# Second attention of a four-layer model: attention outputs and their sums leave PSUM by ACT, are inverted once per sequence on DVE and multiplied on POOL

## The reference, cut to what matters

```python
qkv = x @ w_attn
q = qkv[..., :D].reshape(Bv, Tv, H, HEAD_D).transpose(0, 2, 1, 3)
k = qkv[..., D:D + HEAD_D]
v = qkv[..., D + HEAD_D:]
att = jnp.einsum('bhqd,bkd->bhqk', q, k) * scale
att = jnp.where(causal[None, None, :, :], att, -jnp.inf)
att = jax.nn.softmax(att, axis=-1)
y = jnp.einsum('bhqk,bkd->bhqd', att, v)
y = y.transpose(0, 2, 1, 3).reshape(Bv, Tv, D)
return y @ w_proj
```

## Time and profile before

| | |
|---|---|
| median of 3 runs | 796.57 us (796.4 to 796.59) |
| span of the profiled execution, first to last instruction | 801.9 us; no other time of that execution is listed |
| PE busy / DVE busy | 644.6 us (80%) / 548.5 us (68%) |
| ACT busy / POOL busy | 353.9 us (44%) / 361.2 us (45%) |
| attention turns 1 to 6, from one query product to the next | 37.5 to 37.9 us each |

### The profile page before, as it was taken

How to read it: one execution, slowest core, us unless ns; L and a number is a source line. 1 busy time by engine, 2 the same in 40 slices (tenths; PEclk the granted TensorE clock), 3 DMA queues, 4 the chain that set the end, 5 groups by cost and what they waited for, 6 DMA issues and landing times.

```text
span 801.9 us, 14622 instructions
## 1 busy us (share of the span) xinstructions
PE 644.6 (80%) x4312; PEld 398.9 (50%) x4345; DVE 548.5 (68%) x1808; ACT 353.9 (44%) x764; POOL 361.2 (45%) x513
## 2 busy tenths in 40 slices
PE   1489898997206699999795569899999999999795
PEld 1246666664103478877584223454545454544453
DVE  8378888888691133243336797889898989898454
ACT  0323232320711222233231205776777777767883
POOL 0176555552007587788862102434434344333342
PEclk9999999999657799999997667999999999999998
DMA  9300000000231222223324440203131221300011
GB/s 297 106 1 1 0 1 0 0 1 1 78 106 49 32 43 41 41 42 43 44 25 102 52 59 4 60 16 50 26 41 31 34 41 25 50 15 2 17 54 40
DMA packets 42937, 33.51 MB, mean 42 GB/s; under 512 B 4144, under 2 KB 39520, under 8 KB 42864
## 3 DMA queue, kind: packets, MB, share of 16 engines
q1 hardware_dynamic: 32528, 24.62, 14.3%
q0 software_dynamic: 8992, 7.38, 6.4%
q10 hardware_dynamic: 1344, 0.62, 0.3%
HBM read 13.87 MB, written 8.91 MB: 28 GB/s over the span
## 4 chain that ended last, share of the span: by engine, by line
PE 45%; DVE 20%; POOL 13%; issue 12%; ACT 3%; DMA 2%; SPq 1%; DVEq 0%; ACTq 0%; POOLq 0%
PE bank L1982 8%; DVE masked L1574 7%; POOL x_dram L950 7%; POOL x_row L943 6%; PE wide L1969 5%; PE wide L639 4%; PE bank L1914 3%; PE bank L611 3%; PE wide L640 3%; PE bank L1121 2%; DVE st L292 2%; DVE mx L1574 2%; DVE prod L389 2%; PE wide L621 1%; PE bank L1994 1%
## 5 line engine op out<-in xcount | busy, mean ns | idle before, releaser
L1761 ACT ACTIVATE pexp<-wide 128x512 f32<-128x512 f32 (+2 forms) x384 | 181.3, 535 | 73.4 <-PE wide L1969 70.2
L1685 POOL TENSOR_SCALAR_AFFINE_SELECT pexp<-pexp 128x256 f32<-128x256 f32 x256 | 106.1, 418 | 185.7 <-ACT pexp L1761 183.7
L1574 DVE CUSTOM_DVE_ANT_0 masked<-bank,mask_qk 128x384 f32<-128x384 f32 (+3 forms) x356 | 154.0, 481 | 18.6 <-PE bank L1914 17.7
L1969 PE MATMUL wide<-qT,kTe 128*128 128x256 bf16 (+3 forms) x501 | 119.7, 301 | 6.6 <-ACT pexp L1761 2.5
L1092 ACT ACTIVATE hT<-wide,b1T 128x512 f32<-128x512 f32 x64 | 43.8, 687 | 147.1 <-PE wide L1112 112.8
L1914 PE MATMUL bank<-kTm,qT 128*128 128x384 bf16 (+3 forms) x348 | 87.1, 318 | 18.9 <-DVE mx L1574 9.4
L950 POOL DMA_INDIRECT x_dram<-yg,row_u x48 | 76.2, 1588 | 31.5 <-DVE yg L999 18.6
L1574 DVE CUSTOM_DVE_ANT_0 masked<-wide,mask_qk 128x256 f32<-128x256 f32 (+3 forms) x156 | 74.2, 498 | 17.8 <-PE wide L1914 17.8
L943 POOL DMA_INDIRECT x_row<-xln_dram,row_u x64 | 62.4, 975 | 52.8 <-DVE slot_tok L819 33.6
L1982 PE MATMUL bank<-pexp,vx 128*32 128x512 f32 (+3 forms) x1024 | 83.9, 439 | 0.5 <-POOL pexp L1685 0.5
L1121 PE MATMUL bank<-w_sb,hT 128*128 128x128 f32 x512 | 71.6, 283 | 5.0 <-issue 5.0
(11 more groups left out here) (273 smaller groups left out, 1056.0 us busy)
## 6 DMA issues: line engine op xcount, KB each, us to landing
qT<-qp SPq DMA_DIRECT2D x144, 64.0 KB
x_sb<-in_L_attn_x SPq DMA_DIRECT2D x8, 256.0 KB, 6.7
w_sb<-in_L_ffn_w SPq DMA_DIRECT2D x1, 2048.0 KB, 13.3
xln_dram<-rx SPq DMA_DIRECT2D x8, 256.0 KB, 2.3
out_x<-x_sb SPq DMA_DIRECT2D x7, 256.0 KB, 2.3
x_dram<-x_sb SPq DMA_DIRECT2D x6, 256.0 KB, 3.6
x_sb<-x_dram SPq DMA_DIRECT2D x6, 256.0 KB, 2.8
x_row<-xln_dram,row_u POOLq DMA_INDIRECT x64
```

The source lines that it names most:

```text
L1574: ins = nc.vector.tensor_tensor_reduce(out=masked[:, n % 4, at], in0=bank_of(n)[:, at], in1=mask_qk[:, T - w:T], scale=1.0, scalar=LEAST, ...
L1685: nc.gpsimd.affine_select(out=pexp[:, at, :, 0:P], in_=pexp[:, at, :, 0:P], pattern=[[0, 2], [1, P]], compare_op=ALU.is_ge, fill=0.0, base ...
L1761: nc.scalar.activation(pexp[:, exp_slot(b, 2 * step + h // 2), h % 2:h % 2 + nh, 0:w], scores_bank(b, m)[:, 0:nh * w].rearrange("p (h t) - ...
L1969: ins = nc.tensor.matmul(scores_bank(b, m)[:, hh * w:(hh + 1) * w], kTe[:, par, j * P:(j + 1) * P], qT[:, b % QB, 4 * qd + h + hh, j * P:T ...
```

## The change

For the tails in the loop (sequences 0 to 6) the divide is spread over three engines. `act_back` copies the 16 x 9 outputs and sums of a tile from `psT` to an SBUF tile `y_sum`; it stands in ACT's list in steps 0 to 3 right after the exponentials of the next step. `pe_back` of the next tile waits for that copy and no longer for `y2`. When all four copies are there, `dve_sums_inverse` inverts the 64 sums of the sequence in one operation (step 4 A), and `pool_divide` multiplies all 512 outputs in one operation, ahead of POOL's two selects of step 4. `pe_yT` moves from step 4 D to step 5 B.

```diff
-        q_oTp, q_rd, q_y = Q("o_back_psum", NT), Q("sum_inverse", NT), Q("y", NT)
+        q_oTp, q_rd, q_y = Q("o_back_psum", NT), Q("sums_inverse"), Q("y")
+        q_ys = Q("y_and_sum", NT)
...
-        TAIL = Tail({(0, "D"): 0, (1, "D"): 1, (2, "D"): 2, (3, "D"): 3}, {(1, "A"): 0, (2, "A"): 1, (3, "A"): 2, (4, "A"): 3},
-                    (4, "D"), 5, (6, "B"), (RESIDUAL_STEP, "D"), (7, "B"))
+        TAIL = Tail({(0, "D"): 0, (1, "D"): 1, (2, "D"): 2, (3, "D"): 3}, (4, "A"),
+                    (5, "B"), 5, (6, "B"), (RESIDUAL_STEP, "D"), (7, "B"))
...
-        def dve_divide(dve, b, k):
-            dve.wait_ge(q_oTp.sem, q_oTp.at(b, k + 1))
-            ps = psT[:, :].rearrange("p (h c) -> p h c", c=32)
-            nc.vector.reciprocal(rd[:, k % 2, :], ps[:, :, L]).then_inc(q_rd.sem, 1)
-            dve.wait_ge(q_rd.sem, q_rd.at(b, k + 1))
-            dve.wait_ge(q_yTp.sem, q_yTp.at(b, 0))
-            nc.vector.tensor_tensor(y2[:, k, :].rearrange("p (h l) -> p h l", l=L), ps[:, :, 0:L],
-                                    rd[:, k % 2, :].unsqueeze(2).broadcast_to([P, HEADS, L]),
+        def act_back(act, b, k):
+            act.wait_ge(q_oTp.sem, q_oTp.at(b, k + 1))
+            act.wait_ge(q_y.sem, q_y.at(b, 0))
+            nc.scalar.activation(y_sum[:, k], psT[:, :].rearrange("p (h c) -> p h c", c=32)[:, :, 0:L + 1],
+                                 ACT.Copy).then_inc(q_ys.sem, 1)
+
+        def dve_sums_inverse(dve, b):
+            dve.wait_ge(q_ys.sem, q_ys.at(b, NT))
+            dve.wait_ge(q_y.sem, q_y.at(b, 0))
+            nc.vector.reciprocal(rd[:, :, :], y_sum[:, :, :, L]).then_inc(q_rd.sem, 1)
+
+        def pool_divide(pool, b):
+            pool.wait_ge(q_rd.sem, q_rd.at(b, 1))
+            pool.wait_ge(q_yTp.sem, q_yTp.at(b, 0))
+            nc.gpsimd.tensor_tensor(y2[:, :, :].rearrange("p k (h l) -> p k h l", l=L), y_sum[:, :, :, 0:L],
+                                    rd[:, :, :].unsqueeze(3).broadcast_to([P, NT, HEADS, L]),
                                     ALU.mult).then_inc(q_y.sem, 1)
...
-                    if tail and (s, place) in TAIL.divide:
-                        dve_divide(dve, b - 1, TAIL.divide[s, place])
+                    if tail and (s, place) == TAIL.divide:
+                        dve_sums_inverse(dve, b - 1)
...
+                if b and s == TAIL.divide[0]:
+                    pool_divide(pool, b - 1)
...
+                if tail and (s, "D") in TAIL.back:
+                    act_back(act, b - 1, TAIL.back[s, "D"])
...
             if k:
-                pe.wait_ge(q_y.sem, q_y.at(b, k))
+                pe.wait_ge(q_ys.sem, q_ys.at(b, k))
...
-            pe.wait_ge(q_y.sem, q_y.at(b, NT))
+            pe.wait_ge(q_y.sem, q_y.at(b, 1))
```

More of the change, by code:

```diff
@@ L1261, in build @@
         oT = scratch("oT", [P, 2, NQ, T])
-        rd = scratch("rd", [P, 2, HEADS])
+        rd = scratch("rd", [P, NT, HEADS])
+        y_sum = scratch("y_sum", [P, NT, HEADS, L + 1])
         y2 = scratch("y2", [P, NT, D])
@@ L1397, in dve_end_divide @@
             ps = psE_back[k][:, :].rearrange("p (h c) -> p h c", c=32)
-            nc.vector.reciprocal(rd[:, k % 2, :], ps[:, :, L]).then_inc(q_rd.sem, 1)
+            nc.vector.reciprocal(rd[:, k, :], ps[:, :, L]).then_inc(q_rd.sem, 1)
             dve.wait_ge(q_rd.sem, q_rd.at(B - 1, k + 1))
             nc.vector.tensor_tensor(y2[:, k, :].rearrange("p (h l) -> p h l", l=L), ps[:, :, 0:L],
-                                    rd[:, k % 2, :].unsqueeze(2).broadcast_to([P, HEADS, L]),
+                                    rd[:, k, :].unsqueeze(2).broadcast_to([P, HEADS, L]),
                                     ALU.mult).then_inc(q_y.sem, 1)
```

## The result

The changed kernel takes 817.46 us (median of 4 runs, 816.25 to 817.73) where the kernel before takes 796.58 (4 runs, 796.4 to 796.9): 1.0255 times as long, with an interval of 1.0241 to 1.027. Forecast were 811.5 us and a range of 800 to 818.

The account below looks back on a forecast made before the run. In the changed steps PE was taken to bound the kernel, with ACT feeding it just in time and DVE having time to spare. 13.4 + 0.6 + 0.9 = 14.9 us on the timed 796.57 gave 811.5 us, range 800 to 818.

Parts of the forecast that it names:

- Three waits a turn on ACT: Turns 1 to 5: copies waiting for `pe_back` delay `xln`, `xT`, then `qp` and exponentials; 2.68 us a turn, 13.4 in all.
- DVE's relief at nothing: DVE loses 1.64 us of work a turn, costed at nothing: it falls in steps where DVE waits for PE.
- Copy 0.29, inversion 0.54, multiply 1.08 to 1.27: Durations in us taken for ACT's copy, DVE's inversion of 64 sums and POOL's multiply of 512 elements (1.27 used).
- The rival of a multiply twice as long: POOL needs twice 1.27 us: 1.1 us more in turns 1 to 5, 1.3 in turn 7; 819.3 us, chance 0.06.
- Turn 6, 0.6: Turn 6 has no `xln`, `xT` or `qp`; only the last ACT wait bites, delaying `oT`: 0.6 us.
- Turn 7, 0.9: Turn 7, step 5 B: value sums wait for POOL's selects behind the multiply, 0.9 us of PE waiting.
- multiply to 762.41, two selects to 763.25: Turn 7's working: POOL's multiply ends at 762.41, its two selects at 763.25; PE would come at 762.37.
- main case: ACT's waits in turns 1 to 6 plus turn 7's wait: 811.5 us, own range 806 to 817, chance 0.64.

Follow-up runs that it names:

- x3: Kernel before, plus four ACT copies of 144 constants into an unread tile, each waiting for the same `pe_back` as the changed kernel's copies: 811.0 us, 1.0183.
- x4: x3 without the copies' wait for `pe_back`: 799.15 us, 1.0043 of before.
- y2: x3 with the fourth unread copy alone (step 3 only): 800.85 us, 1.0063 of before.
- y3: x3 with the first three unread copies alone (steps 0 to 2): 806.05 us, 1.0131 of before.
- z1: Kernel before with the loop's division left out; DVE copies one column of each tile instead: 796.16 us, 1.0006 of before.
- x2: Changed kernel with POOL's multiply run on DVE, right behind the inversion: 812.11 us, 1.021 of before.
- y4: Changed kernel once more, unaltered, for a second profile: 817.15 us (one run).
- x1: Changed kernel with the four copies behind `xln`, `xT` and `qp` in ACT's list of each step: 805.35 us, 1.0117 of before.
- y1: x1 with the fourth `pe_back` a half-step earlier, `pe_yT` one place later, turn 7's multiply on DVE: 802.5 us, 1.008 of before.

## Why the prediction was right, and what it mis-sized

The mechanism was right, and it is shown by runs: x3 makes the loss of turns 1 to 5 with a wait alone, x4 loses it without the wait, and y2 and y3 split it.

- *Three waits a turn on ACT, 5 x 2.68 = 13.4.* Measured are 2.82 in a turn without half clock, and 13.8 for the five turns. Counted from the start of turn 2 (557.07 before, 551.88 after), the transposes of `xln` move from 12.66 to 13.64 and the query product from 14.33 to 15.92. The score behind the first exponential of step 5 moves from 18.39 to 20.99. These are 0.98, 1.59 and 2.60 late, where 0.95, 1.50 and 2.68 were forecast. The key and value product behind the scores (576.29 before, 573.92 after) is 2.82 late: the last 0.22 comes up only where `pe_yT` has moved behind the scores of step 6. The working put that move at nothing. No run tests it by itself; in x3, which leaves `pe_yT` at its place, the turn is 2.69 longer.
- *DVE's relief at nothing.* z1 shows it for turns 1 to 5. The relief itself was mis-sized: busy time fell by 1.02 us a turn, not 1.64. The durations of DVE's instructions add up to some 1.6 us less, but neighbouring operations overlap. That changes nothing. DVE was busy 33.40 of 37.58 us, yet taking 1.34 us from it gives 1.0006, and the offload itself gives 1.0255. The Trainium skill (Perfetto Trace Analysis, Optimizing Scalar/DVE Operations) says that offloading may make sense if DVE is saturated. By its share of busy time DVE looks saturated here, but the time of a turn doesn't follow its load.
- *Copy 0.29, inversion 0.54, multiply 1.08 to 1.27.* The groups by shape after, ACT, DVE and POOL:

```profile
L1592 ACT ACTIVATE y_sum<-bank 128x144 f32<-128x144 f32 x28 | 8.2, 294 | 20.0 <-PE bank L2008 20.0
```

```profile
L1598 DVE RECIPROCAL rd<-y_sum 128x64 f32<-128x64 f32 x6 | 3.3, 553 | 0.4
```

```profile
L1603 POOL TENSOR_TENSOR y<-y_sum,rd 128x512 f32<-128x512 f32 x6 | 6.5, 1076 | 27.7 <-DVE rd L1598 27.7
```

  0.294, 0.553 and 1.076. The copy lies on the line between 64 and 512 elements, so its strided operand costs nothing visible. The multiply takes what the subtraction of L539 takes. The working read that row as one of plain operands, but L539 broadcasts its second operand over the 8 features of a head as the multiply does, so it was the nearer price. The rival of a multiply twice as long is out in turns 1 to 5, as x2 shows too.
- *Turn 6, 0.6:* 0.71 measured, but the nearness is luck. The wait is worth 0.54 (y2's turn 6 takes 36.18). POOL's multiply is not covered here: x2's turn 6 takes 36.03, 0.32 less than the changed kernel's. DVE's relief gives 0.35 back (z1). The working had the last two at nothing, and they nearly cancel; some 0.2 is left, as much as the move of `pe_yT` in turns 1 to 5.
- *Turn 7, 0.9: mis-sized.* Without half clock turn 7 is 2.01 longer (y4). The step that failed is the sum "multiply to 762.41, two selects to 763.25", which took its durations from rows of other stretches. Here POOL runs beside the normalisation of an earlier sequence's filter on DVE. Timelines of POOL and DVE, turn 7 after (the last two rows of DVE, from earlier in the turn, have no operation of POOL beside them):

```profile
772.60 1.39 POOL L1603 TENSOR_TENSOR y<-y_sum,rd 128x512 f32<-128x512 f32 x1 [3.85 <-DVE rd L1598]
773.94 0.86 POOL L1695 TENSOR_SCALAR_AFFINE_SELECT pexp<-pexp 128x256 f32<-128x256 f32 x1
...
774.75 0.85 POOL L1695 TENSOR_SCALAR_AFFINE_SELECT pexp<-pexp 128x256 f32<-128x256 f32 x1
```

```profile
772.43 0.63 DVE L1348 TENSOR_TENSOR fx<-x_sb,mv 128x512 f32<-128x512 f32 x1
773.09 1.44 DVE L1350 TENSOR_TENSOR fx<-fx,rstd 128x512 f32<-128x512 f32 x1
774.45 0.89 DVE L1351 TENSOR_TENSOR x_sb<-x_sb,fb_sb 128x512 f32<-128x512 f32 x1
775.26 0.67 DVE L1357 TENSOR_TENSOR x_sb<-x_sb,bank 128x512 f32<-128x512 f32 x1
...
759.08 0.69 DVE L1350 TENSOR_TENSOR fx<-fx,rstd 128x512 f32<-128x512 f32 x1
759.69 0.68 DVE L1351 TENSOR_TENSOR x_sb<-x_sb,fb_sb 128x512 f32<-128x512 f32 x1
```

  The multiply reads 1.39 (0.12 over the 1.27 taken), the two selects 0.86 and 0.85 instead of 0.42 each (0.87 over). That makes 0.9 + 0.12 + 0.87 = 1.9 of the 2.01. It is for these selects that PE waited 1.82 us. The trace of the kernel before shows such a pair already. In its turn 7 a select beside the same filter on DVE takes 0.79:

```profile
755.98 0.79 POOL L1685 TENSOR_SCALAR_AFFINE_SELECT pexp<-pexp 128x256 f32<-128x256 f32 x1 [0.36 <-ACT pexp L1761]
```

- *The clock: not in the forecast.* Three stretches at half clock in the first profile lengthen turns 2, 5 and 7 by 1.62, 1.65 and 1.58 us; the second profile has one in turn 3 and another behind turn 7, in the last sequence's own tail (stage view of y4, granted clock 0.55):

```profile
797.00:800.80 3.80, 3.80 (x20) 3.80 (x21) 1.80 (x7) 1.55 (x4) 1.27 (x1) 0.55 0.00 0
```

  The tail is 1.50 longer there than in the first profile. Without half clock the turns make 13.8 + 0.7 + 2.0 = 16.5 us, the first profile's stretches 4.8 more: 21.3 over the turns. The runs show 20.9. How many stretches the other timed executions hold is not known, so this last step of the sum is open by some 1.6 us for each one more or fewer.
- *The range.* 817.46 lies half a microsecond inside the range of 800 to 818 and outside the main case's own 806 to 817. The upper end was drawn for a late multiply, and what filled it was the clock. Without half clock the sum gives 796.58 + 16.5 = 813.1. That the mechanism held is no luck; that the time stayed inside the range is in part.

## What to carry to other kernels

An operation handed to an engine with time to spare can cost by its place in that engine's list and not by its busy time: ask what the new operation waits for and what stands behind it. Here four copies of some 0.3 us cost 0.24 us a turn without their wait and 2.69 with it. A busy share near the top does not make an engine the bound; if it idles for another one beside the work to be moved, moving the work may pay nothing, as here. Take durations from rows with the same neighbours on the other engines: DVE's and POOL's prices for an operation alone did not hold side by side.

## What the runs showed of the hardware

**POOL and DVE take turns.** In the two timelines of turn 7 above each operation with all operands in SBUF that starts beside one of the other engine ends about its own lone duration after that one ends. The multiply, alone 1.08, ends 0.93 after L1348 (773.06, 773.99); L1350, alone 0.69, ends 0.54 after the multiply (774.53); the first select, 0.42, ends 0.27 after L1350 (774.80); L1351, alone 0.68, ends 0.54 after that select (775.34); the second select ends 0.26 after L1351 (775.60). The Trainium skill (SBUF — State Buffer, SBUF: two separate sides) has a rule for this: a DVE operation with two SBUF inputs and a GpSimd operation that reads SBUF share one pair of ports, the first holds it for its whole instruction and the other is blocked. The trace agrees, but for 0.14 to 0.16 us of each operation that evidently overlaps. L1357, which reads one operand from PSUM, takes 0.67 (775.26) with selects running beside it, so the rule's condition on the operands fits as well. No run was made to test the rule by itself.

**Half clock in the middle of the loop.** The stage view of the changed kernel, the three stretches and a plain one of turn 3; the column behind POOL is PE's granted clock:

```profile
575.00:578.60 3.60, 3.60 (x21) 0.85 (x20) 0.78 (x4) 1.20 (x3) 2.05 (x9) 0.56 0.57 77
597.00:600.60 3.60, 3.60 (x39) 1.65 (x32) 3.03 (x12) 2.79 (x7) 1.17 (x3) 1.00 0.05 14
697.00:700.50 3.50, 3.50 (x23) 1.54 (x26) 1.26 (x5) 1.49 (x4) 2.00 (x7) 0.59 0.52 78
761.50:766.00 4.50, 4.34 (x21) 1.96 (x22) 1.09 (x2) 3.13 (x8) 1.66 (x4) 0.62 0.00 0
```

The clock falls to its lower level, 1.2 of 2.4 GHz, for most of each stretch, though PE is busy for all but 0.16 us of the three together. In turns 1 to 5 this came in the changed kernel (three times in two profiles) and in x2 (once, turn 3), each time some 23 us into the turn, about 2 us behind PE's three waits for ACT. In the kernels without the first two of these waits (before, x1, x4, y1, y2, z1) it did not come there; in x3 and y3, which have them, it did not either. In turn 7 it came in x1, x4, y1 and y3 as well, so that one can't be put down to the change. What sets it off stays open.
